# A hint for the instruction fetch at the head of each engine's loop, in an attention and SwiGLU kernel

## The reference

```python
xn = _layernorm(x, axis=-1)
x = x + attention(xn, Wq, bq, Wk, bk, Wv, bv, Wo, bo) + ffn(xn, w_gate, w_up, w_down)

# attention: q, k with rotary embedding, k and v repeated for the 4 heads of a group
scores = jnp.einsum('bthd,bshd->btsh', q, k) * scale
probs = jax.nn.softmax(scores, axis=2)
context = jnp.einsum('btsh,bshd->bthd', probs, v).reshape(b, t, DIM)
return context @ Wo.T + bo

# ffn
h = jax.nn.silu(gate) * up
return jnp.einsum('bsh,dh->bsd', h, wd)
```

## Time and profile before

| | |
|---|---|
| median of 3 runs | 840.81 us (837.9 to 842.76) |
| the profiled execution | 837.63 us |
| its span, first to last instruction | 835.6 us |
| mean granted TensorE clock | 0.971 of full speed |
| TensorE matmuls busy | 746.2 us (89%) |
| VectorE busy | 729.0 us (87%) |
| ScalarE busy | 595.8 us (71%) |
| GpSimd busy | 110.6 us (13%) |

### The profile page before, as it was taken

One profiled execution on the slowest core, in us unless ns is written; L12 is line 12 of the kernel. 1 busy time (PEld: TensorE's weight loads), 2 busy tenths in 40 slices (PEclk: granted clock), 3 DMA queues, 4 the chain that ended last, 5 costly groups with the idle time before them and its releaser, 6 DMA issues.

```text
span 835.6 us, 18056 instructions
## 1 busy us (share of the span) xinstructions
PE 746.2 (89%) x4856; PEld 239.4 (29%) x4856; DVE 729.0 (87%) x1363; ACT 595.8 (71%) x1171; POOL 110.6 (13%) x205
## 2 busy tenths in 40 slices
PE   4597999989998999989998999979998899999996
PEld 2221232323232232323232232323232232323252
DVE  7597999979998899979998899969998999999831
ACT  2432778867876778867876778857886778877864
POOL 3155433407000000000000000000000000000000
PEclk9796999999999899999999899999999999999999
DMA  6301221212110001111110001111010111110021
GB/s 204 90 4 48 55 63 30 68 32 66 30 29 21 19 22 30 28 31 29 30 29 21 20 21 30 28 31 29 23 36 10 28 24 29 29 29 1 2 64 38
DMA packets 29220, 30.35 MB, mean 36 GB/s; under 512 B 6672, under 2 KB 21264, under 8 KB 29008
## 3 DMA queue, kind: packets, MB, share of 16 engines
q1 hardware_dynamic: 27552, 25.05, 11.0%
q0 software_dynamic: 720, 2.36, 1.0%
q10 hardware_dynamic: 864, 2.15, 0.7%
HBM read 23.12 MB, written 6.03 MB: 35 GB/s over the span
## 4 chain that ended last, share of the span: by engine, by line
PE 63%; DVE 18%; issue 9%; ACT 6%; SPq 1%; DMA 1%; DVEq 1%; ACTq 0%
PE acc_ps L934 24%; PE banks L848 17%; DVE mx L686 15%; PE banks L865 8%; PE banks L940 5%; ACT probs L532 5%; PE banks L949 3%; PE banks L957 2%; PE banks L818 1%; PE banks L974 1%; PE banks L824 1%; DVE gated L732 1%; DMA y_all<-in_x 1%; ACT th L581 0%; PE banks L965 0%
## 5 line engine op out<-in xcount | busy, mean ns | idle before, releaser
L686 DVE TENSOR_REDUCE mx<-banks 128x1 f32<-128x512 f32 x1024 | 632.9, 683 | 47.2 <-PE banks L848 31.2
L532 ACT ACTIVATE probs<-banks 128x512 f32<-128x512 f32 x1024 | 541.9, 601 | 170.9 <-PE banks L865 150.1
L848 PE MATMUL banks<-ka,qa 48*128 48x512 bf16 x1024 | 301.2, 390 | 36.1 <-DVE mx L686 21.3
L865 PE MATMUL banks<-qc,kc 51*128 51x512 bf16 x1024 | 313.0, 387 | 17.8 <-ACT probs L532 13.8
L934 PE MATMUL acc_ps<-probs,v_grp 128*32 128x512 f32 x2048 | 276.0, 612 | 0.0
L848 PEld LDWEIGHTS banks<-ka,qa 48*128 48x128 bf16 x1024 | 77.3, 94 | 352.6 <-DVE mx L686 286.3
L865 PEld LDWEIGHTS banks<-qc,kc 51*128 51x128 bf16 x1024 | 76.1, 94 | 78.9 <-ACT probs L532 74.7
L418 POOL TENSOR_TENSOR neg_max<-row_max,nought 128x16 bf16<-128x16 f32 x31 | 6.9, 222 | 510.1 <-DVE row_max L692 510.1
L934 PEld LDWEIGHTS acc_ps<-probs,v_grp 128*32 128x32 f32 x2048 | 40.6, 108 | 59.0 <-issue 46.1
L940 PE MATMUL banks<-xn_T,w_ffn 128*128 (+1 forms) x192 | 54.3, 405 | 1.3
L940 PEld LDWEIGHTS banks<-xn_T,w_ffn 128*128 128x128 f32 x192 | 32.6, 189 | 24.8 <-DVE mx L686 15.2
(11 more groups left out here) (90 smaller groups left out, 266.7 us busy)
## 6 DMA issues: line engine op xcount, KB each, us to landing
qa<-q_parts SPq DMA_DIRECT2D x32, 96.0 KB
qc<-q_parts SPq DMA_DIRECT2D x64, 48.0 KB
q_parts<-part POOLq DMA_DIRECT2D x9, 256.0 KB, 3.7
y_all<-in_x SPq DMA_DIRECT2D x4, 512.0 KB, 9.7
qa<-q_parts SPq DMA_DIRECT2D x32, 64.0 KB
qc<-q_parts SPq DMA_DIRECT2D x64, 32.0 KB
out<-y_all SPq DMA_DIRECT2D x8, 256.0 KB, 2.3
ka<-k_parts SPq DMA_DIRECT2D x32, 48.0 KB
```

The costliest lines, as they stand in the source:

```text
L532: nc.scalar.activation(probs[:, s % SLOTS, j, :], banks[:, score_bank(G * s + j), :], ACT.Exp, scale=SCALE).then_inc(exp_done, 1)
L686: nc.vector.tensor_reduce(out=mx[:, h, col, k:k + 1], in_=ps, op=ALU.max, axis=AX.X).then_inc(max_done, 1)
L848: nc.tensor.matmul(ps, qa[par][rows, j // 2, t * P:(t + 1) * P], ka[par][rows, k * W:(k + 1) * W], start=True, stop=True).then_inc(a_ready, 1)
L865: nc.tensor.matmul(banks[:, score_bank(u), :], kc[par][rows, kt * P:(kt + 1) * P], qc[par][rows, h, j // 2, :], start=True, stop=True).the ...
```

## The change

Each of the five loops is opened through `nc.Fori` with the engine named and `hint_back_edge=True`, instead of through the engine's own `Fori`. The loops run over the same range with the same bodies. [...]

```diff
-            with sp.Fori(0, NG // 2 - 1) as pair:
+            with nc.Fori(0, NG // 2 - 1, engines=[sp.engine], hint_back_edge=True) as pair:
                 group(pair * 2, 0, 3)
                 group(pair * 2 + 1, 1, 3)
...
-            with pool.Fori(0, NG // 2 - 3) as pair:
+            with nc.Fori(0, NG // 2 - 3, engines=[pool.engine], hint_back_edge=True) as pair:
...
-            with act.Fori(0, NG // 2 - 1) as pair:
+            with nc.Fori(0, NG // 2 - 1, engines=[act.engine], hint_back_edge=True) as pair:
...
-            with dve.Fori(0, NG // 2 - 1) as pair:
+            with nc.Fori(0, NG // 2 - 1, engines=[dve.engine], hint_back_edge=True) as pair:
...
-            with pe.Fori(0, NG // 2 - 1) as pair:
+            with nc.Fori(0, NG // 2 - 1, engines=[pe.engine], hint_back_edge=True) as pair:
```

## The result

The changed kernel takes 809.72 us (median of 4, 808.33 to 811.24) against 839.79 before (837.9 to 842.76): a ratio of 0.9639, 95% interval 0.9604 to 0.9674. Its profiled execution took 809.95 us, with a span of 808.1; before it was 837.63 and 835.6.

What follows compares the result with a forecast made beforehand. TensorE and VectorE alternate with little slack, and missing code stops VectorE and ScalarE at six jumps. Profiled 837.6 - 30.9 (jumps) + 0.7 (hint) = 807.4 us; half the median's 3.2 excess gives 809, range 803 to 840.

Steps and rivals of the forecast that it cites:

- The sum's main term: ScalarE's and VectorE's six jumps back: head code present at each jump saves 30.9 us, 5.1 a jump (563.9 - 533.0).
- the control across the fall-through: At the loop's end without a taken jump, group marks lie 44.40 us apart, so passing it without a jump costs nothing.
- the forecast's last step: Run median 3.2 us above the profiled execution, partly perhaps more slow-clock jumps (some 2 us each); half taken, giving 809.
- The sign given: Inside the loop, no stretch at clock 0.50 would remain if the forecast was right.
- The hint's own price: One added instruction at each body's head, may show on TensorE: 0.1 us x 7 passes = 0.7 us, bounds 0 and 1.7.
- the 88.9 to 89.3 us given as a sign: Length of a loop pass expected if the forecast was right.
- The 0.23 us in front of TensorE's first weight load: TensorE's wait after the branch, taken or not; expected to remain, about 0.23 us, if the forecast was right.
- The exit: Seventh pass, where the hint is wrong: a late line could cost up to 6.6 us; taken as 0.
- Rival (a): Hint at the body's top acts too early, head thrown out later by straight-on fetches: no gain, 838.3 us; chance 14%.
- Rival (b): At the jumps, fetch starts late or serves one of two engines: partial gain, 826 us, from 815 to 836; chance 10%.
- Rival (c): Head's line displaces one in VectorE's or ScalarE's body, stopping all seven passes: +5.5 us, 843, or 874; chance 6%.

## Why the prediction was right, point by point

**What a jump costs.** The sum's main term was 30.9 us for six jumps, from the group marks and the control across the fall-through the earlier trace rows; measured 31.1. One reading under it was off by a little: 754.84 is a start from the timeline and 710.44 one from the chain, which has it 0.07 late. Like for like the fall-through's stretch is 44.47 us, not 44.40, before and after the change; the 44.43 of the even-to-odd step and the sum stand. The waits by themselves would have given 14.0 or 20.5, and it was right not to use them: the pauses of the two engines overlap, and yet each stretch grows by 4.0 us or more, where the longest pause is 3.7, and three of them have the low clock on top.

**The slow clock.** Before, the three dearer stretches are those with a mean granted clock under 1.00 (0.96, 0.96 and 0.98), and in one of them it stood at 0.50 for 6.82 us. They took 284.90 - 3 x 93.00 = 5.9 us more than the other three, the 2 us each of the forecast's last step. The sign given was that no stretch at 0.50 is left in the loop, and none is: none of the six has a mean under 1.00. In the kernel with the hint on ScalarE alone the clock fell to half after every jump, for 3.4 us or so each time, and there a jump still costs 3.2 us.

**The hint's own price.** Predicted 0.7 us, bounds 0 and 1.7; measured 31 to 61 ns an instruction and nothing on the path: 88.80 us a stretch is no more than 2 x 44.42 = 88.84, and the three engines' hints alone gave a ratio of 1.0004. The term was too large by all of it, and the stretches lie just under the 88.9 to 89.3 us given as a sign. The 0.23 us in front of TensorE's first weight load stayed, as said.

**The exit.** This is the step of the sum that failed. I took 0, since a line lasts 39 us and 24 us would be left after the fall-through to fetch the next. The fetch did not use them. In the changed kernel q14 moves nothing from 680 to 700 us and its four packets between 730 and 750, when ScalarE runs out of code. My reading is that a hint of "taken" in the last pass holds the straight-on fetch back, and that falling through doesn't set it going again: nothing on q14 from ScalarE's branch at 706.6 us to 740. The kernel that turns the hint to "not taken" moves two packets between 680 and 700 us, ahead of the exit, and has no late line. Measured 2.5 us in the profiled execution (1.3 in the one where the clock stayed up), within the bound of 6.6. The arithmetic of the line is not what failed; that the fetch unit starts again at the branch was assumed.

**The median.** For the profiled execution the sum gave 807.4, and 809.95 came: -0.7 for the hint, +2.6 behind the loop, nearly all of it the exit, +1.0 ahead of the loop, -0.2 for the jumps and -0.2 for the time around the span (2.0 before, 1.8 after) make the +2.5. The 809 was 1.6 above the sum for the median, half of a difference that I couldn't place. That it came within 0.7 of 809.7 is partly luck: the hint and the 1.6 us without a place were put too high, the exit too low. The 30.9 us for the jumps is the part that was right by its working.

**Rival (a), the hint does nothing,** is out: 31 us are gone, and in the four-group body the hint stands some 180 us ahead of the jump and changes what is fetched (two q14 packets behind the jump instead of six). At a jump of the kernels without a hint on VectorE and ScalarE and with a body of two or four groups, each of the two stands for 2.2 to 3.7 us, with packets on q14 (six in 18 us). A rival that no run tests is that one more instruction in VectorE's and ScalarE's bodies shifts the code against the fetched lines, whatever the instruction says. The kernel that changes the hint's outcome in the last pass and loses the late line speaks against it, and so does the gain with two lengths of body.

**Rival (b), part of it,** was mispriced. One engine cured was put at 1 us a jump for either. It is 0 for VectorE and 1.6 ((839.2 - 829.6) / 6) for ScalarE, with the exit's price already taken off; at the jumps alone it is 5.1 - 3.2 = 1.9 by the profiles. The idle times of the earlier trace rows don't show that the first job behind the jump needs both engines in turn.

**Rival (c), the stop moves into the body,** didn't happen: the earlier trace rows had spoken against it, and once hinted the loop of two groups fetches nothing at all from its second pass on.

**What I had not asked** is how much of the body could stay. Rival (a) has the straight-on fetches throw the head out, but I took the ten packets a pass for code that must be brought. In the hinted loop the whole body of two groups fits, since q14 is silent from 172 to 700 us. What threw it out, by this, are fetches ahead into the code behind the loop, which six times of seven wasn't needed; the packets don't name their code, so that last step is inferred.

## What to carry to other kernels

A piece of "issue" of 2 to 4 us on an engine at its loop's first line, with packets on the instruction queue around it, was missing code in this kernel; price it by the distance of equal marks across the jump and across the fall-through, not by the pause. The cure was a hint on the engines that stop, or a shorter body (here one group instead of two: the same time without any hint). The hinted loop paid once at its exit (1.3 to 2.6 us with ScalarE's hint, nothing with VectorE's alone), some 35 us behind the branch in the body of two groups, so look there; a hint that says "not taken" in the last pass removed it.

## What the runs showed of the hardware that I had not expected

- The hint took fetches away rather than adding to them: 72 packets on q14 become 12, and a body of four groups has 10 packets a pass instead of 14, two right after the jump instead of six.
- After the fall-through against the hint, the changed kernel's q14 moved nothing for 33 us (706.6 to 740), then ScalarE stood 1.75 us in "issue" while four packets came.
- Where the two engines stopped together, the one with less work (ScalarE, 71% busy against 87%) set the price: its stop alone cost 5.9 us a jump, as much as both together in an execution with a like clock; VectorE's alone cost 3.2.
- VectorE's code written out instead of looped made each group 0.14 us shorter (44.26 against 44.40); ScalarE's, on top of it, 0.38 longer (44.64). VectorE written out and ScalarE on single groups gave the shortest median of all, 805.92 us.
